# First expert stage of a two-layer gated block: lower half with stationary weights, results turned back later

## The reference, cut to what matters

```python
exp_batches = jnp.einsum('tec,td->ecd', sec_mask, xt)          # rows of each expert
h = jax.nn.gelu(jnp.einsum('ecd,edf->ecf', exp_batches, c_fc), approximate=False)   # upper half, 256 -> 1024
exp_out = jnp.einsum('ecf,efd->ecd', h, c_proj)                # lower half, 1024 -> 256
out = cb_weight.reshape(T, N_EXP * cap) @ exp_out.reshape(N_EXP * cap, d)
```

## Time and profile before

| | us |
|---|---|
| median of three runs | 1591.28 |
| lowest and highest | 1584.92, 1595.44 |
| profiled execution, device time | 1582.21 |
| its span, first to last instruction | 1580.5 |
| mean granted TensorE clock | 0.933 |
| PE busy | 1321.9 |
| DVE busy | 871.5 |
| ACT busy | 809.9 |

### The profile page before, as it was taken

How to read it: one execution, slowest core, us unless ns; L and a number is a source line. 1 busy time by engine, 2 the same in 40 slices (tenths; PEclk the granted TensorE clock), 3 DMA queues, 4 the chain that set the end, 5 groups by cost and what they waited for, 6 DMA issues and landing times. The chain is left out here.

```text
span 1580.5 us, 36281 instructions
## 1 busy us (share of the span) xinstructions
PE 1321.9 (84%) x10688; PEld 1043.2 (66%) x10689; DVE 871.5 (55%) x2881; ACT 809.9 (51%) x2219; POOL 434.2 (27%) x810
## 2 busy tenths in 40 slices
PE   5898888988279999359999999989999999449992
PEld 3666566666168888357778777878787777326661
DVE  4666566666245454446566676666675767222223
ACT  4777667677136455345565555556564555113332
POOL 6334555443502313010012213121212121312221
PEclk9999999999689999769999999999999999669996
DMA  7941313210134440220000000000000013311114
GB/s 213 361 145 66 105 51 105 95 64 12 35 133 155 145 152 27 97 84 12 12 12 12 21 11 22 11 21 11 22 10 22 0 38 161 117 32 60 60 60 138
DMA packets 45589, 114.97 MB, mean 73 GB/s; under 512 B 8876, under 2 KB 29036, under 8 KB 41808
## 3 DMA queue, kind: packets, MB, share of 16 engines
q1 hardware_dynamic: 37444, 95.62, 18.1%
q0 software_dynamic: 7168, 14.99, 2.9%
q10 hardware_dynamic: 880, 3.28, 0.6%
HBM read 70.42 MB, written 47.65 MB: 75 GB/s over the span
## 5 line engine op out<-in xcount | busy, mean ns | idle before, releaser
L774 ACT ACTIVATE b_prob<-b_prob,b_low 100x361 f32<-100x361 f32 x256 | 154.9, 605 | 100.6 <-DVE b_low L886 98.5
L623 PE MATMUL b_ps_p<-b_context_part,b_wk_part 128*128 128x362 f32 x768 | 157.7, 342 | 0.0
L782 ACT COPY b_prob_t<-b_ps_t 128x300 f32<-128x300 f32 x256 | 103.5, 404 | 104.9 <-PE b_ps_t L687 101.8
L1471 ACT ACTIVATE a_prob<-a_prob,a_low 100x361 f32<-100x361 f32 x256 | 153.4, 602 | 0.4 <-DVE a_low L1614 0.4
L629 PE MATMUL b_ps_p<-b_wv_part,b_context_part 128*128 128x512 f32 (+1 forms) x576 | 151.6, 406 | 0.0
L1479 ACT COPY a_prob_t<-a_ps_t 128x300 f32<-128x300 f32 x256 | 97.4, 407 | 105.0 <-PE a_ps_t L1374 86.9
L886 DVE CUSTOM_DVE_ANT_0 b_prob<-b_ps_s,b_mask_bias 100x361 f32<-100x361 f32 x256 | 121.4, 530 | 37.1 <-PE b_ps_s L677 21.6
L1614 DVE CUSTOM_DVE_ANT_0 a_prob<-a_ps_s,a_mask_bias 100x361 f32<-100x361 f32 x256 | 121.4, 531 | 29.7 <-PE a_ps_s L1364 23.7
L687 PE MATMUL b_ps_t<-ident,b_prob 100*128 100x100 f32 x768 | 117.6, 262 | 24.0 <-ACT b_prob_t L782 23.8
L623 PEld LDWEIGHTS b_ps_p<-b_context_part,b_wk_part 128*128 128x128 f32 x768 | 124.8, 190 | 0.3 <-issue 0.3
L687 PEld LDWEIGHTS b_ps_t<-ident,b_prob 100*128 100x128 f32 x768 | 78.8, 142 | 66.9 <-issue 50.8
(11 more groups left out here) (301 smaller groups left out, 2664.6 us busy)
## 6 DMA issues: line engine op xcount, KB each, us to landing
rows_in<-zero SPq DMA_DIRECT2D x44, 514.0 KB, 5.9
w<-in_c_fc SPq DMA_DIRECT2D x8, 1024.0 KB, 7.1
w<-in_c_proj SPq DMA_DIRECT2D x8, 1024.0 KB, 5.3
a_context<-in_ctx SPq DMA_DIRECT2D x16, 361.0 KB, 3.5
b_context<-in_ctx SPq DMA_DIRECT2D x16, 361.0 KB
rows_in<-rows_in SPq DMA_DIRECT2D x8, 514.0 KB, 5.1
f_xe<-rows_in SPq DMA_DIRECT2D x8, 514.0 KB
f_xe<-rows_in SPq DMA_DIRECT2D x32, 128.5 KB, 2.1
```

The costliest lines, as they stand in the source:

```text
L623: ins = nc.tensor.matmul(bank[:, 0:LN2], w_parts["k"][a][:, k, t * P:(t + 1) * P], cx_parts[s][b][:, k, :], start=m == 0, stop=m == DK * l ...
L774: nc.scalar.activation(prob[0:S, k, 0:L], prob[0:S, k, 0:L], ACT.Exp, bias=low[0:S, k:k + 1], scale=-1.0, accum_out=total[0:S, k:k + 1]).t ...
L1471: nc.scalar.activation(prob[0:S, k, 0:L], prob[0:S, k, 0:L], ACT.Exp, bias=low[0:S, k:k + 1], scale=-1.0, accum_out=total[0:S, r:r + 1]).t ...
```

## The change

The lower half is computed the other way round. A 128x128 piece of `w2_parts` is stationary and the 512 rows of `ht` stream, so that there are two blocks (of output columns) of 24 matmuls with 512 columns in place of four blocks with 256. The result has output columns on partitions, in banks `ps[4]` and `ps[5]`. DVE copies each to a new tile `yt[d]` (128x512). PE turns the two tiles back with eight 128x128 transposes, into `ps[6]` and `ps[7]`, two to a block of rows, and DVE copies the four blocks to `ye[s]`. This happens in the next expert's upper half: on PE after block f = 1, on DVE after the subtraction of block f = 0. The last expert's results are turned at the end. PE's and DVE's first iteration are written out, since expert 0 has no one before it. ACT, POOL and SP keep their instructions; waits on `down_done` count two instead of four.

```diff
-                for j in range(4):
-
-                    pe.wait_ge(y_ready.sem, y_ready.at(i, s * 4 + j - 1))
+                for d in range(DK):
+
+                    pe.wait_ge(yt_ready.sem, yt_ready.at(i, DK * (s - 1) + d + 1))
                     for m, (f, (a, b)) in enumerate((f, ab) for f in range(NF) for ab in PASSES):
-                        if j == 0 and m % len(PASSES) == 0:
+                        if d == 0 and m % len(PASSES) == 0:
                             pe.wait_ge(h_ready.sem, h_ready.at(i, s * NF + f + 1))
                             if f % (NF // 2) == 0:
                                 pe.wait_ge(w2_ready.sem, w2_ready.at(i, 2 * s + f // (NF // 2) + 1))
-                        ins = nc.tensor.matmul(ps[4 + j % 2][:, 0:D], ht[a][:, f, j * P:(j + 1) * P], w2_parts[b][:, f, :],
+                        ins = nc.tensor.matmul(ps[4 + d][:, :], w2_parts[b][:, f, d * P:(d + 1) * P], ht[a][:, f, :],
                                                start=m == 0, stop=m == NF * len(PASSES) - 1)
                     ins.then_inc(down_done.sem, 1)
...
+            def turn_back(i, s):
+
+                pe.wait_ge(yt_ready.sem, yt_ready.at(i, DK * (s + 1)))
+                for j in range(4):
+                    pe.wait_ge(y_ready.sem, y_ready.at(i, s * 4 + j - 1))
+                    for d in range(DK):
+                        ins = nc.tensor.transpose(ps[6 + j % 2][:, d * P:(d + 1) * P], yt[d][:, j * P:(j + 1) * P], T["ident"][:, :])
+                    ins.then_inc(y_turned.sem, 1)
...
                     ins.then_inc(up_done.sem, 1)
+                    if f == 1 and behind:
+                        turn_back(i if s else i - 1, 1 - s)
...
+            def take_results(i, s):
+                for j in range(4):
+                    dve.wait_ge(y_turned.sem, y_turned.at(i, s * 4 + j + 1))
+                    if j == 0 and not (isinstance(i, int) and i == 0):
+
+                        dve.wait_ge(y_out[s], 64 * i)
+                    nc.vector.tensor_copy(ye[s][:, j, :], ps[6 + j % 2][:, 0:D]).then_inc(y_ready.sem, 1)
...
                     nc.vector.tensor_tensor(ht[1][:, f, :], hidden[f % NH][:, :], ht[0][:, f, :],
                                             ALU.subtract).then_inc(h_ready.sem, 1)
+                    if f == 0 and behind:
+                        take_results(i if s else i - 1, 1 - s)
...
-                for j in range(4):
-                    dve.wait_ge(down_done.sem, down_done.at(i, s * 4 + j + 1))
-                    if j == 0 and not (isinstance(i, int) and i == 0):
-
-                        dve.wait_ge(y_out[s], 64 * i)
-                    nc.vector.tensor_copy(ye[s][:, j, :], ps[4 + j % 2][:, 0:D]).then_inc(y_ready.sem, 1)
-                    if j == 0 and more:
+                for d in range(DK):
+                    dve.wait_ge(down_done.sem, down_done.at(i, DK * s + d + 1))
+                    dve.wait_ge(y_turned.sem, y_turned.at(i, s * 4))
+                    nc.vector.tensor_copy(yt[d][:, :], ps[4 + d][:, :]).then_inc(yt_ready.sem, 1)
+                    if d == 0 and more:
                         next_weights(i, s, 1)
...
+            turn_back(E // 2 - 1, 1)
```

More of the change, by code:

```diff
@@ L1918, in experts_first @@
     ht = [sb(f"ht{k}", [P, NF, SLOTS], F32R) for k in range(2)]
+    yt = [sb(f"yt{k}", [P, SLOTS]) for k in range(DK)]
     ye = [sb(f"ye{s}", [P, 4, D]) for s in range(2)]
@@ L1933, in experts_first @@
     h_ready = Counted(nc, nm + "h_ready", 2 * NF)
-    down_done = Counted(nc, nm + "down_done", 8)
+    down_done = Counted(nc, nm + "down_done", 2 * DK)
+    yt_ready = Counted(nc, nm + "yt_ready", 2 * DK)
+    y_turned = Counted(nc, nm + "y_turned", 8)
     y_ready = Counted(nc, nm + "y_ready", 8)
@@ L1996, in upper_weights @@
                 pool.wait_ge(w_in[s], 32 * (i + 1))
-                pool.wait_ge(down_done.sem, down_done.at(i, 4 * s))
+                pool.wait_ge(down_done.sem, down_done.at(i, DK * s))
                 apart(pool)
@@ L2036, in _ @@
         def _(pe):
-            for k in (x_turned, up_done, down_done):
+            for k in (x_turned, up_done, down_done, y_turned):
                 k.credit(pe)
@@ L2048, in turn, with step @@
                 ins.then_inc(x_turned.sem, 1)
-            def step(i, s, more, two):
+            def turn_back(i, s):
[5 more added lines that the diff above has]
+                    ins.then_inc(y_turned.sem, 1)
+            def step(i, s, more, behind):
                 pe.wait_ge(xt_ready.sem, xt_ready.at(i, s))
@@ L2074, in _ @@
             turn(1, 0, xt_ready.before(0))
-            experts(pe, step)
+            for s in range(2):
+                step(0, s, True, s > 0)
+            with pe.Fori(1, E // 2 - 1) as i:
+                for s in range(2):
+                    step(i, s, True, True)
+            for s in range(2):
+                step(E // 2 - 1, s, s == 0, True)
+            turn_back(E // 2 - 1, 1)
             for q in range(Norm.GROUPS):
@@ L2105, in upper @@
                 def upper(f):
-                    act.wait_ge(down_done.sem, down_done.at(i, s * 4))
+                    act.wait_ge(down_done.sem, down_done.at(i, DK * s))
                     act.wait_ge(gelu_done.sem, gelu_done.at(i, s * NF + f + 1))
@@ L2141, in _ @@
         def _(dve):
-            for k in (xt_ready, w1_ready, w2_ready, h_ready, y_ready):
+            for k in (xt_ready, w1_ready, w2_ready, h_ready, yt_ready, y_ready):
                 k.credit(dve)
@@ L2184, in _ @@
             for s in range(2):
-                step(0, s, True, True)
+                step(0, s, True, s > 0)
             with dve.Fori(1, E // 2 - 1) as i:
@@ L2189, in _ @@
             for s in range(2):
-                step(E // 2 - 1, s, s == 0, False)
+                step(E // 2 - 1, s, s == 0, True)
+            take_results(E // 2 - 1, 1)
             combine(dve)
```

## The result

The changed kernel takes 1607.24 us (median of 4 runs, 1605.62 to 1610.12), the kernel before 1589.13 (4 runs, the three of the table above and one more, 1584.92 to 1595.44). The medians differ by 18.1 us, or 1.1%. The ratio measured is 1.0132, which would be 21 us, with a 95% interval of 1.0102 to 1.0161: the changed kernel is slower by 1.0 to 1.6%. Forecast were 1611 us and +20.

What follows compares the result with a forecast made beforehand. PE, 84% busy, was taken to bound the kernel. Lower halves -12.3, turning back +20.7, end +3.1 and five clock falls 8.5 gave +20.0 us: 1602.2 on the profiled execution, 1611 on the median, range 1596 to 1620.

Steps and rivals of the forecast that it cites:

- Lower half, 10.92 us: PE's lower half per expert: 48 matmuls of 512 columns at 0.2275 us, 10.92 in place of 12.67; 0.68 less work.
- w2's wait: Thirteenth lower-half matmul waiting for DVE's second subtraction of w2: 1.07 us goes; in the last expert 0.58 stays.
- The turn, 3.07 us: Transposes in the next upper half: f = 2 starts at 5.80 us, not 2.73; 0.78 work, 2.3 idle; 20.7 lost in all.
- The end: After the last expert, DVE copies, PE turns, POOL issues four DMAs in a row: +3.1 us, with 1.96 gained already in it.
- The clock: PE's clock after idle time in seven upper halves: five falls to half speed, 1.7 us each, 8.5 us.
- The 2.14 us: PE's idle time in one piece in each of seven upper halves, compared with earlier idle times that held or fell.
- Sum: All terms in the expert stage and its end: +11.5 us with the clock up, +20.0 with five falls.
- the clock holds: Rival: no fall in any of the seven upper-half gaps; +11.5 us, 0.7%, 1603 on the median; chance 0.26.
- The hidden turn: Rival: DVE's first copy starts early enough that PE loses only 0.78 us in five upper halves; -5.3 us, 1586; chance 0.09.

Runs made afterwards that it cites:

- w2 early: Kernel before with one number changed: DVE makes the second half of w2's lower part after block 5 of the hidden tile, not 6; 0.52% under the kernel before.
- filling the gap: Changed kernel plus seven unneeded 512-column matmuls between the second and third transpose pairs in seven upper halves; stage 9.6 us shorter than the changed kernel's 215.4.
- The filled gaps: Changed kernel plus three unneeded 512-column matmuls, not seven, between the second and third transpose pairs, leaving 1.12 and 1.60 us idle; stage 205.7 us.
- two blocks to a bank: Changed kernel with two blocks of rows turned into each of banks 6 and 7 instead of one; 0.13% under the kernel before, interval including no change.

## Why the prediction was right

- *Lower half, 10.92 us.* 10.98 to 11.01 in the changed kernel: with `ht` streaming the form has the upper half's pace within 1%. The old form without its wait takes 11.59 (w2 early), so the work saved is 0.6 us a lower half, where 0.68 was forecast. By the formula of the Trainium skill ("TensorE: Matmul & The Clock Gate", section "Back-to-back issue gap") it would have been an estimated 0.1 us: the measurement decides against it.
- *w2's wait.* Gone in seven experts. In the last PE waits to 3.31 us after its start, the very number of the earlier trace rows:

```profile
653.17 2.88 PE L2084 MATMUL f_ps<-f_ht,f_w_part 128*128 128x512 f32 x12
656.48 8.42 PE L2084 MATMUL f_ps<-f_ht,f_w_part 128*128 128x512 f32 x36 [0.43 <-DVE f_w_part L2196]
```

- *The turn, 3.07 us.* f = 2 at 5.66 in place of 5.80, at 6.14 in place of 6.28 with the table load. Most of the 0.14 is the hand-over from DVE to PE, 0.06 us where the prediction had 0.14. The second wait, after the third pair, is there though no row shows it as idle time: the fourth pair starts 0.33 us after the third, as DVE's copies do, and 0.34 was forecast; pairs that wait for nothing start 0.22 apart. From the start of the last transpose ahead of the gap (477.28) to the next (479.37) are 2.09 us.
- *The end.* The stretch behind the last matmul grew by 5.7 us; the forecast had 5.1 (the 3.1, and the 1.96 of the last lower half that it had taken off).
- *The clock.* Six falls, not five, 1.62 us each (27.34 less 25.72) against 1.7. That idle time lets the clock fall, and what a fall costs, was right; filling the gap shows it. The number of falls was chosen between none and seven by the length of the gap, and that reasoning does not hold, so that it came within one is luck. The 2.14 us were reckoned from starts, the 1.72 and 1.73 that had held are idle times as the profile gives them; by that measure the gap is 1.81 us, hardly longer, and in the two experts with the table load 2.30, which the prediction had as 2.14 too. And the length alone does not settle it. In the attention of the kernel before, after the first of these waits the clock stayed at 1.00, and from 1.2 us after the second it was at 0.50 for 3.4 us:

```profile
54.04 0.45 PE L1374 MATMUL a_ps_t<-ident,a_prob 100*128 100x100 f32 x3 [1.83 <-ACT a_prob_t L1479]
...
129.68 0.45 PE L1374 MATMUL a_ps_t<-ident,a_prob 100*128 100x100 f32 x3 [1.72 <-issue]
```

  The very wait of the earlier trace rows that had held, 1.73 us at 402.71, was followed by a fall in the execution of the changed kernel, where the same eight matmuls take 2.81 us in place of 1.94 (a timeline row, then a stretch):

```profile
406.72 2.81 PE L1336 MATMUL a_ps_p<-wo,a_out_t 128*100 128x256 f32 x8 [1.71 <-DVE a_out_t L1631]
...
407.65:411.05 3.40, 1.89 (x5) 0.85 (x3) 1.29 (x3) 0.00 (x0) 1.43 (x2) 0.50 0.26 76
```

  The filled gaps show 1.12 and 1.60 to be harmless in this stage.
- *Sum.* Stage and end rose by 21.9 us against 20.0. Small errors partly cancel in it: the lower halves saved 0.6 less than forecast in all, the end cost 0.6 more and the falls 1.2 more, and turning back cost 0.9 less up to f = 2 (5 x 2.93 and 2 x 2.55, 19.8). The profiled execution took 1606.6 against 1602.2: it also began the stage 4.2 us later than that of before, which the change has no part in, and its span has 2.0 less behind stage and end. The median is 1607 and not 1611 for two reasons: the kernel before has a lower median with its fourth run, 1589.1, and the two medians lie only 18.1 apart.
- *Rivals.* That the clock holds was 0.26: filling the gap shows what it would have given, 0.8%, against 0.7% forecast. The hidden turn, -5.3 us, is near what two blocks to a bank brings about: -3.3 in stage and end. For it to be faster by over 1% the prediction asks for 0.21 us a matmul; its own terms give 0.20 (0.2275 less 10.6 / 384).

## What to carry to other kernels

Ask of every wait for a buffer not whether its user is quick, but what stands ahead of it in that engine's order: the copy took 0.42 us, but PE's transposes stood still for 2.1, since ahead of the copy was a subtraction that waited for ACT. Before rebuilding a stage for its pace, look at which part of it is a wait; here the wait was 1.07 of the 1.75 us that the swap could give, and moving one instruction by one place took it without any turning back. And a gap on PE has two prices, its length and what the clock does after it; the second can be seen by filling it with work that nobody needs. When idle times are compared, as here with those after which the clock held, they have to be read in the same way, and one case that held is no bound.

## What the runs showed of the hardware

- In this stream of 512-column matmuls, idle times of 1.81 and 2.30 us were followed by 3.4 us at 1.2 GHz in 12 of 14 cases; idle times of 1.12 and 1.60 us in none of 7. Each low stretch cost 1.6 us.
- Among the small matmuls of the attention, one and the same wait of 1.7 us was followed by a fall in one execution and not in another (406.72 in the changed kernel, 402.71 in that before).
- 96 matmuls of 256 columns take 11.59 us and 48 of 512 columns 10.98, for the same product: the wider form is only 5% quicker.
- A copy of 128x512 from PSUM takes DVE 0.69 us, of 128x256 0.42; two in a row of the latter 0.75.
- Eight 128x128 transposes of float32 in a row take PE 0.79 us (493.60 to 494.39 with two blocks to a bank).
